# The second layer's softmax placed in the last seven turns of the gathering stage, one step per engine and turn

## The reference

```
def gat_conv(x, src, dst, W, a_src, a_dst, b, num_nodes):
    h = jnp.einsum('nd,dhf->nhf', x, W)
    al_s = jnp.sum(h * a_src, axis=-1)
    al_d = jnp.sum(h * a_dst, axis=-1)
    logits = jax.nn.leaky_relu(al_s[src] + al_d[dst], NEG_SLOPE)
    m = jax.ops.segment_max(logits, dst, num_segments=num_nodes)
    e = jnp.exp(logits - m[dst])
    z = jax.ops.segment_sum(e, dst, num_segments=num_nodes)
    alpha = e / (z[dst] + 1e-16)
    msg = h[src] * alpha[..., None]
    out = jax.ops.segment_sum(msg, dst, num_segments=num_nodes)
    return out.reshape(num_nodes, -1) + b
...
h = gat_conv(x, src, dst, W1, a_src1, a_dst1, b1, n)    # 8 heads
out = gat_conv(h, src, dst, W2, a_src2, a_dst2, b2, n)  # 1 head
```

## Time and profile before

| | |
|---|---|
| median of three runs | 3975.6 us |
| the profiled execution, its time | 3978.42 us |
| its span in the profile | 3976.6 us |
| PE, DVE, ACT, POOL busy over the span | 82%, 71%, 48%, 57% |
| mean granted TensorE clock | 0.919 of full speed |
| gathers of `gather_out1` (L595) | 100, mean 1094 ns |

### The profile page before, as it was taken

The page is one execution under the profiler, slowest core; times in us unless marked ns, Lnnn a source line. Parts: engine busy times, 40 slices in busy tenths (PEclk is TensorE's granted clock), DMA queues, the critical chain, the costliest instruction groups (busy, mean ns, idle before and its releaser), DMA issues. The chain is left out here.

```text
span 3976.6 us, 57087 instructions
## 1 busy us (share of the span) xinstructions
PE 3270.6 (82%) x14868; PEld 2599.0 (65%) x14868; DVE 2815.4 (71%) x7915; ACT 1892.1 (48%) x5401; POOL 2282.9 (57%) x2529
## 2 busy tenths in 40 slices
PE   5999926687675998469999972999999999999775
PEld 4888725575464665237777761878878787878654
DVE  5767668697784666875666651888888888888633
ACT  3777615576232111233333330566656665666455
POOL 4766500587475664133333321878788787878577
PEclk8999959899898999559999995999999999999898
DMA  4887739443574332463333329767767676767654
GB/s 144 245 247 242 225 113 367 128 131 109 153 218 128 93 88 60 140 200 96 114 113 113 111 87 323 228 200 234 227 205 235 201 233 199 233 198 233 188 189 156
DMA packets 690470, 710.73 MB, mean 179 GB/s; under 512 B 73444, under 2 KB 644190, under 8 KB 689796
## 3 DMA queue, kind: packets, MB, share of 16 engines
q1 hardware_dynamic: 592204, 484.13, 39.3%
q0 software_dynamic: 68288, 181.26, 16.1%
q10 hardware_dynamic: 29660, 41.70, 3.1%
HBM read 427.77 MB, written 296.22 MB: 182 GB/s over the span
## 5 line engine op out<-in xcount | busy, mean ns | idle before, releaser
L595 POOL DMA_INDIRECT s_i_messages<-h,table_row x600 | 645.6, 1076 | 192.2 <-issue 81.5
L2610 PE MATMUL s_i_bank<-s_i_messages,s_i_equal 128*128 128x256 f32 x1200 | 363.5, 386 | 78.0 <-DMA s_i_messages<-h,table_row 74.1
L776 PE MATMUL s_n_bank<-w,n_xt 128*128 128x256 f32 x1280 | 308.1, 384 | 21.4 <-DMA n_xt<-in_x_t 21.4
L2647 DVE SCALAR_TENSOR_TENSOR s_i_y<-s_i_bank,s_i_scale,s_i_acc 128x256 f32<-128x256 f32 x600 | 284.5, 475 | 44.1 <-PE s_i_bank L2610 24.5
L794 PE MATMUL s_n_bank<-w_out,n_ht 128*128 128x256 f32 x1280 | 309.9, 386 | 0.9 <-ACT n_ht L804 0.9
L785 PE MATMUL s_n_bank<-n_x3t,w_in 128*128 128x256 f32 x1280 | 304.1, 381 | 0.0
L816 ACT ACTIVATE n_w<-n_w,n_small 128x256 f32<-128x256 f32 x320 | 145.1, 500 | 308.1 <-POOL n_small L843 307.4
L2610 PEld LDWEIGHTS s_i_bank<-s_i_messages,s_i_equal 128*128 128x128 f32 x1200 | 218.6, 193 | 108.5 <-issue 79.5
L776 PEld LDWEIGHTS s_n_bank<-w,n_xt 128*128 128x128 f32 x1280 | 247.2, 193 | 56.7 <-DMA n_xt<-in_x_t 21.8
L794 PEld LDWEIGHTS s_n_bank<-w_out,n_ht 128*128 128x128 f32 x1280 | 247.6, 194 | 36.0 <-ACT n_ht L804 1.3
L785 PEld LDWEIGHTS s_n_bank<-n_x3t,w_in 128*128 128x128 f32 x1280 | 244.3, 191 | 33.9 <-ACT n_x3t L674 0.2
(11 more groups left out here) (426 smaller groups left out, 9401.6 us busy)
## 6 DMA issues: line engine op xcount, KB each, us to landing
h<-s_i_y SPq DMA_DIRECT2D x600, 128.0 KB, 3.2
n_xt<-in_x_t SPq DMA_DIRECT2D x160, 256.0 KB
out<-n_w SPq DMA_DIRECT2D x160, 256.0 KB, 2.2
s_i_equal<-eq_tab SPq DMA_DIRECT2D x600, 64.0 KB
x<-s_x_rows SPq DMA_DIRECT2D x100, 256.0 KB
out<-s_a_hs SPq DMA_DIRECT2D x100, 128.0 KB
proj_dst<-s_a_hd SPq DMA_DIRECT2D x100, 128.0 KB
h<-s_h_rows SPq DMA_DIRECT2D x50, 256.0 KB, 4.0
```

The lines of the kernel that those rows point to most:

```text
L595: return net.nc.gpsimd.indirect_dma_start(out, None, table, bass.IndirectOffsetOnAxis(index, 0))
L776: mm = self.nc.tensor.matmul(self.pr[:, g * self.D:(g + 1) * self.D], self.XT[u][:, c, g * P:(g + 1) * P], self.net.w12[:, c, :], start=c ...
L2610: nc.tensor.matmul(banks[r % 4][:, 0:D], EQ[q % NM][:], M[q % NM][:], start=True, stop=True).then_inc(summed, 1)
L2647: V.scalar_tensor_tensor(Y[q % NY][:], banks[r % 4][:, 0:D], scale[:, s, t:t + 1], acc[:, t, :], ALU.mult, ALU.add).then_inc(added, 1)
```

## The change

`softmax(net, 2)` as a stage of its own is gone. Its instructions now stand in `gather_out1`, in a class `Softmax2`, at the heads of the last seven turns (START = 34 to 40): one step on an engine in a turn, ahead of what the dense chain has in that turn. Its `Segments` has two PSUM banks instead of four, and its transposes another two. For this `Segments`' sum and maximum are cut in two, at the question to TensorE. The table `at` spreads the 100 gathers over the gaps of the first 34 turns instead of all 41. The arithmetic is the same.

```
 class Segments:
-    def __init__(self, net, st, H):
+    def __init__(self, net, st, H, banks=4):
...
-        self.bank = st.ps("seg_bank", 4)
+        self.bank = st.ps("seg_bank", banks)
+        self.half = banks // 2
...
     def _ask(self, ch):
         ch.wait()
         ch.eng.sem_inc(self.ask, 1)
         self.asked += 1
+
+    def _answer(self, ch):
         ch.eng.wait_ge(self.got, self.asked)
...
     def sum_dve(self, ch, tot, val, n):
+        self.sum_begin(ch, tot, val, n)
+        self.sum_end(ch, tot, n)
...
+class Softmax2:
...
+    def rows(self, pe, dots_ready, value):
+        pe.wait_ge(dots_ready, value)
+        T = self.net.T
+        for k in range(5):
+            mm = self.nc.tensor.transpose(self.bank[k // 4][0:T, k % 4 * P:(k % 4 + 1) * P], self.net.dots2[:, k, :], self.net.ident[:])
+        mm.then_inc(self.rows_ready, 1)
+
+    def cols(self, pe):
+        T = self.net.T
+        pe.wait_ge(self.w_ready, 1)
+        for i, buf in enumerate((self.L, self.S)):
+            mm = self.nc.tensor.transpose(self.bank[0][:, i * T:(i + 1) * T], buf[:], self.net.ident[0:T, 0:T])
+        mm.then_inc(self.cols_ready, 1)
...
+    def move_rows(self, act):
+        T = self.net.T
+        act.wait_ge(self.rows_ready, 1)
+        self.nc.scalar.activation(self.dots[:, 0:4 * P], self.bank[0][0:T, :], ACT.Copy)
+        self.nc.scalar.activation(self.dots[:, 4 * P:5 * P], self.bank[1][0:T, 0:P], ACT.Copy).then_inc(self.rows_moved, 1)
+
+    def exps(self, act):
+        act.wait_ge(self.exp_ask, 1)
+        self.nc.scalar.activation(self.S[:], self.S[:], ACT.Exp)
+        self.nc.scalar.activation(self.L[:], self.L[:], ACT.Exp).then_inc(self.exp_done, 1)
...
+    def sums_begin(self, dve):
+        self.ch = Chain(dve, self.chain)
+        dve.wait_ge(self.rows_moved, 1)
+        self.seg.sum_begin(self.ch, self.W, self.dots[:, P:3 * P], 2)
+
+    def logits(self, dve):
+        V, ch, L, S, W, dots, T = self.nc.vector, self.ch, self.L, self.S, self.W, self.dots, self.net.T
+        self.seg.sum_end(ch, W, 2)
...
+        self.seg.max_begin(ch, W, L, 1)
+
+    def differences(self, dve):
+        V, ch, L, S, W = self.nc.vector, self.ch, self.L, self.S, self.W
+        self.seg.max_end(ch, W, 1)
...
+        dve.sem_inc(self.exp_ask, 1)
+
+    def totals_begin(self, dve):
+        dve.wait_ge(self.exp_done, 1)
+        self.ch(self.nc.vector.memset(self.L[:, 0:1], 0.0))
+        self.seg.sum_begin(self.ch, self.W, self.L, 1)
+
+    def weights(self, dve):
+        V, ch, L, S, W = self.nc.vector, self.ch, self.L, self.S, self.W
+        self.seg.sum_end(ch, W, 1)
...
+        dve.sem_inc(self.w_ready, 1)
...
 def gather_out1(net):
...
+        sm = Softmax2(net, st)
         TURNS = dn.units + 5
-        GAPS = TURNS * dn.PIECES
-        at = {t * (GAPS - CHUNK) // T: t for t in range(T)}
+        GAPS = (TURNS - 7) * dn.PIECES
+        at = {t * (GAPS - 8) // T: t for t in range(T)}
+        START = TURNS - 7
...
         @block.tensor
         def _(pe):
             for i in range(TURNS):
+                if i == START:
+                    sm.rows(pe, dot, T)
+                if i == START + 1:
+                    sm.seg.cross_pe(pe, 2, False)
+                if i == START + 2:
+                    sm.seg.cross_pe(pe, 1, True)
+                if i == START + 4:
+                    sm.seg.cross_pe(pe, 1, False)
+                if i == START + 5:
+                    sm.cols(pe)
                 dn.turn_pe(pe, i // 2, i % 2, none)
...
         @block.scalar
...
+                if i == START:
+                    sm.move_rows(act)
+                if i == START + 3:
+                    sm.exps(act)
+                if i == START + 6:
+                    sm.move_cols(act)
                 dn.turn_act(act, i // 2, i % 2)
...
         @block.vector
...
+                if i == START + 1:
+                    sm.sums_begin(dve)
+                if i == START + 2:
+                    sm.logits(dve)
+                if i == START + 3:
+                    sm.differences(dve)
+                if i == START + 4:
+                    sm.totals_begin(dve)
+                if i == START + 5:
+                    sm.weights(dve)
                 dn.turn_dve(dve, i // 2, i % 2, gap)
...
                 gather_out1(net)
-                softmax(net, 2)
                 gat2(net)
```

More of the change, by code:

```diff
@@ L201, in cross_pe @@
             nc.tensor.matmul(bank[0][0:T, 0:n], net.upper[:], self.ends[:, 0, 0:n], start=True, stop=True)
-            mm = nc.tensor.matmul(bank[2][0:T, 0:n], net.lower[:], self.ends[:, 1, 0:n], start=True, stop=True)
+            mm = nc.tensor.matmul(bank[self.half][0:T, 0:n], net.lower[:], self.ends[:, 1, 0:n], start=True, stop=True)
         else:
@@ L230, in sum_dve, with sum_end @@
         self._ask(ch)
+    def sum_end(self, ch, tot, n):
+        T, net, nc, m = self.T, self.net, self.net.nc, n * P
+        V = nc.vector
+        self._answer(ch)
         for i in range(2):
-            ch(V.tensor_copy(self.cross[:, i, 0:n], self.bank[2 * i][0:T, 0:n]))
+            ch(V.tensor_copy(self.cross[:, i, 0:n], self.bank[self.half * i][0:T, 0:n]))
         ch.wait()
@@ L1197, in softmax @@
     nc, T, H = net.nc, net.T, net.H
-    n = 1 if layer == 2 else H
-    own = layer != 3
+    n = H
+    own = layer == 1
     m = n * P
@@ L1216, in _ @@
         def _(pe):
-            if layer == 2:
-                for k in range(5):
-                    mm = nc.tensor.transpose(bank[k // 4][0:T, k % 4 * P:(k % 4 + 1) * P], net.dots2[:, k, :], net.ident[:])
-                mm.then_inc(rows_ready, 1)
-                seg.cross_pe(pe, 2, False)
-            else:
-                k_all = 2 * H if own else H
-                for b in range(k_all // 4):
-                    for k in range(4):
-                        row, out = 4 * b + k, bank[b][0:T, k * P:(k + 1) * P]
-                        if layer == 1 and row < H:
-                            nc.tensor.matmul(out, net.scores[:, row, :], net.ident[:], start=True, stop=False)
-                            mm = nc.tensor.matmul(out, net.scores[:, 4 * H + row, :], net.ident[:], start=False, stop=True)
-                        else:
-                            mm = nc.tensor.transpose(out, net.scores[:, row, :], net.ident[:])
-                    mm.then_inc(rows_ready, 1)
+            k_all = 2 * H if own else H
+            for b in range(k_all // 4):
+                for k in range(4):
+                    row, out = 4 * b + k, bank[b][0:T, k * P:(k + 1) * P]
+                    if layer == 1 and row < H:
+                        nc.tensor.matmul(out, net.scores[:, row, :], net.ident[:], start=True, stop=False)
+                        mm = nc.tensor.matmul(out, net.scores[:, 4 * H + row, :], net.ident[:], start=False, stop=True)
+                    else:
+                        mm = nc.tensor.transpose(out, net.scores[:, row, :], net.ident[:])
+                mm.then_inc(rows_ready, 1)
             seg.cross_pe(pe, n, True)
@@ L1264, in _ @@
             ch = Chain(dve, chain)
-            if layer == 2:
-                dve.wait_ge(rows_moved, 1)
-                seg.sum_dve(ch, W, dots[:, P:3 * P], 2)
-                ch.wait()
-                ch(V.tensor_tensor(W[:, 0:2 * P], W[:, 0:2 * P], dots[:, 3 * P:5 * P], ALU.add))
-                ch.wait()
-                ch(V.scalar_tensor_tensor(L[:, 0:P], dots[:, 0:P], net.b1_dot[0:T, :], W[:, 0:P], ALU.add, ALU.add))
-                ch(V.scalar_tensor_tensor(S[:, 0:P], W[:, 0:P], net.b1_dot[0:T, :], W[:, P:2 * P], ALU.add, ALU.add))
-            else:
-                dve.wait_ge(rows_moved, (2 * H if own else H) // 4)
+            dve.wait_ge(rows_moved, (2 * H if own else H) // 4)
             for buf in (L, S) if own else (L,):
```

70 lines of the change are left out of this document (57 added, 13 removed).

## The result

The changed kernel has a median of 3988.43 us (9 runs, 3984.03 to 3995.49) against 3973.98 of the kernel before beside it (9 runs, 3966.18 to 3982.41): ratio 1.0035, 95% interval 1.0026 to 1.0045. Timed again later (`after_again`) it was 1.0024, interval 1.0014 to 1.0033. The mean of both, some 0.29%, is 12 us slower.

A forecast was written before the change was run, and what follows sets the result against it. It took a 6.2 us loop over three engines to bound the last seven turns, POOL turns with three gathers. -23.1 + 7.9 + 19.9 + 4.4 = +9.1 us on the median 3975.6 gave 3984.7; range 3974 to 3992.

The forecast's parts named there:

- forecast case: Whole kernel: the likeliest outcome, slower by +5 to +12 us; chance 0.45.
- dear end: Rival, last turns: TensorE at 1.2 GHz from turn 35 to the last store, +12 to +17 us; chance 0.20.
- Removed, -23.1: Softmax stage, 993.48 to 1016.60: it goes, -23.1 us; the 8.03 us before it stay while the last store lands.
- The gathers, +7.9: First 34 turns: denser gathers on POOL; +6.5 in turns 5 to 31, +2 before, -0.6 in 32 and 33.
- cheap bound: Turns 5 to 31: three gathers take 6.64 us a turn as in the diffusion, 183.0 us in all, +3.1.
- Shared interface: POOL in the gather turns: sharing SBUF with VectorE, a late POOL meets other VectorE instructions, to either side; no size.
- The steps, +19.9: Turns 34 to 40: softmax steps at the heads of turns lengthen the tail from 36.2 to 56.0 us.
- the clock, +4.4: TensorE in the tail: four restarts after idling, half of each at the slow level, about 1.1 us each.
- The waits: TensorE near 4 us in turn 35, above 6 in 36; var_5 for squares; out_project(33) for silu; POOL almost none.
- The table: ScalarE, turn 37: Silu's table load after Exp costs 1.28 us by the row; the skill's 2.66 would add 1.4.
- The cheap one: Rival: POOL falls into the diffusion's pattern and TensorE's clock stays up, 0 to +5 us; chance 0.27.
- Steps fill VectorE's idleness: Rival, tail: steps fit VectorE's gaps, VectorE busy 42.2 us, tail grows by 6, kernel -9.2 us; chance 0.08.

The follow-up runs named there:

- pe_late: The changed kernel with only TensorE's combinations and columns moved behind the dense work of their turn; from turn 34's transposes to the last store 49.98 us against 60.33.
- both_late: The changed kernel with TensorE's combinations and columns and ScalarE's exponentials behind the dense work of their turn; ratio 1.0008 to the kernel before, tail 51.27 us.
- warm: The changed kernel with matmuls whose results nothing reads filling TensorE's waits in turns 35, 36, 37 and 39; tail 53.50 us against 60.33, clock 0.98.
- behind: The kernel before with the second softmax in the gathering stage's program behind its last turn, gathers over 41 turns; ratios 0.9985 and 0.9983.
- the best mixture: Softmax mostly behind the last turn, six gathers in the first two gaps, sums_begin and logits behind turns 38 and 39; ratio 0.9983 to the kernel before.

## Why the prediction was right

It gave 3984.7 us and +9.1; the change costs 9.9 and 8.2 where it acts in two pairs of executions, and 0.35% and 0.24% in the medians, which makes 14 and 10 us. The second lies in the forecast case (+5 to +12); the first lies, as a number, in the band of the dear end (+12 to +17), whose mechanism did not come.

- **Removed, -23.1.** Measured: last store to next stage 8.06 against 31.15 (1016.60 less 985.45), -23.09. The landing stayed in full, as said.
- **The gathers, +7.9.** Measured +8.7 to the end of third_norm of turn 33 (957.82 less 724.09, against 949.27 less 724.24). By its parts: turns 0 to 4 +1.9 (forecast +2), turns 5 to 31 took 187.57 (forecast 186.5), turns 32 and 33 gave back 0.8 (0.6). The turns with three gathers average 6.77, as taken, between the two bounds; those with four took 8.44, 8.30 and 8.30 where 8.02 was reckoned. The experiment on them alone gave 8.3. That the middle was hit so closely is in part luck: the same 27 turns took 183.53 in `pe_late`, near the cheap bound's 183.0, and 188.05 in `both_late`.
- **Shared interface.** The Trainium skill, "GPSIMD Engine Reference", section 1, "Specifications", states that GpSimd shares its SBUF interfaces with VectorE and contends with instructions of two SBUF inputs. The prediction reasoned from it that a late POOL meets other VectorE instructions, to either side. The durations of the first pair do move to either side: pow_1 became shorter (mean 1174 ns against 1352), pow_5 and the gathers longer (788 against 754, 1115 against 1096). But in `pe_late` the gathers are shorter than before (1072), and no run isolates contention as the cause.
- **The steps, +19.9, and the clock, +4.4.** Their sum was to make a tail of 60.4 from the third_norm, and it measured 60.4. The split was off, and `warm` shows it: 2.4 less for the steps at full clock (53.59 against 56.0), 2.4 more for the clock (6.8 against 4.4). Both were mis-sized, and that the errors cancel is luck.

| from transposes to transposes | forecast, full clock | `warm` | changed kernel |
|---|---|---|---|
| turn 34 | 10.75 | 10.26 | 12.32 |
| turn 35 | 12.7 | 12.01 | 12.83 |
| turn 36 | 5.6 | 5.66 | 6.11 |
| turn 37 | 11.9 | 11.52 | 13.32 |
| to the last store | 14.7 | 14.05 | 15.75 |

The forecast added the steps' times one behind the other; four of the five stretches came out 0.4 to 0.7 shorter. For the clock it let half of each restart run slow (1.1 each); after the first wait all of project did (3.76), and after the third all of out_project (3.78), 1.9 lost in that group alone. The tail of `after_again` is 59.00, so the 6.8 is uncertain by about 1.3.
- **The waits** came as named: 4.03 in turn 35, 6.80 in turn 36, var_5 behind ScalarE's squares (2.56), silu behind a table load, var_5 no longer waited for by POOL.
- **The table**, 1.28 by the row against about 2.66 with its drain by the Trainium skill, "ScalarE: Activation LUTs", section "What ACT_TABLE_LOAD costs": the run without it gained 1.42 in its turn, so the row's price held, and the whole did not become 1.4 longer, as it would have by the Trainium skill. The Trainium skill, on the same page, section "Table sets: the hidden batching unit", says to batch calls by set; the trace agrees in kind, at about half the price, as only the load back to Silu is on the path.
- **The rivals.** The cheap one needed three gathers at 6.64 and a clock that stays up; the tail's clock fell to 0.79. "Steps fill VectorE's idleness" needed a cross answerable when TensorE gets to it; `pe_late` makes it so and still has a tail of 49.98 against the 42 of that rival; what TensorE waits for there is third_norm, which stands behind VectorE's steps. (The 42.2 counted VectorE's dots, 4.8 us, which the change moves out of the tail; VectorE is busy 37.42 there, and the rival's tail should have been nearer to that.) So a better order took the loss away and did not win: `both_late` is +1.2 where it acts, its interval 1.0 to 1.0017, and `pe_late` about level. The dear end did not come: the clock rose again in every turn (hidden takes 1.89 us in turns 35 and 36, out_project in turn 38).

What stays open: why the first timing reads 14 and the second 10 (their intervals overlap), why the first 34 turns take 3 to 4 us less in some profiles, what the 16 us are that the tail keeps in `pe_late`, and whether later stages take back some 5 us in `behind`.

## What to carry to other kernels

A step of a serial chain that waits for another engine costs less behind a loop's own work in an in-order queue than ahead of it, since the answer may be ready when the queue gets there: on TensorE that was worth some 10 of 26 us here, on ScalarE nothing that can be told from scatter; look for the first instruction that waits and count what is queued behind it. Before spreading such a chain, ask what else it could run beside: here the 8 us of the last store's landing were idle, and the softmax left whole, behind the last turn of the same stage, did as well in the medians as the best mixture and, where it acts, better than every version with all steps in turns 34 to 40 (280.71 and 281.48 us against 287.91 to 302.24). And when a table of slots is compressed to make room, price the compression: it cost about 8 us in the compressed turns, a third of the 23.1 that the removed stage gave, and returned 1.9 of it in the turns that it emptied.
